# Sums of the exponentials in a local attention: from a VectorE pass to ScalarE's accumulator output

## The reference, cut to what matters

```python
def local_attention(q, k, v):            # WINDOW = 64, QK_SCALE = 8
...
    sim = jnp.einsum('bhwid,bhwjd->bhwij', bq, bk)
    mask = (i < j) | (i > j + WINDOW) | (j == -1)
    sim = jnp.where(mask, -jnp.finfo(sim.dtype).max, sim)
    attn = jax.nn.softmax(sim, axis=-1)
    out = jnp.einsum('bhwij,bhwjd->bhwid', attn, bv)
def _layer(x, ...):
    q, k, v = jnp.split(shift_token(x) @ wqkv, 3, axis=-1)   # then heads
    q, k = rotary_xpos(l2norm(q) * qs, l2norm(k) * ksc)
    x = x + local_attention(q, k, v) @ wo
    h = layernorm(shift_token(x)) * lg + lb
    a, g = jnp.split(h @ w1 + b1, 2, axis=-1)
    return x + (a * gelu(g)) @ w2 + b2
```

## Time and profile before

| | us |
|---|---|
| median of 3 runs | 4474.85 |
| lowest, highest | 4472.83, 4477.2 |
| the profiled execution's own time | 4476.7 |
| its span in the trace | 4475.0 |
| mean granted TensorE clock | 0.975 of full speed |

### The profile page before, as it was taken

One profiled execution on the slowest core, in us unless ns is written; L12 is line 12 of the kernel. 1 busy time (PEld: TensorE's weight loads), 2 busy tenths in 40 slices (PEclk: granted clock), 3 DMA queues, 4 the chain that ended last, 5 costly groups with the idle time before them and its releaser, 6 DMA issues. The chain is left out here.

```text
span 4475.0 us, 110467 instructions
## 1 busy us (share of the span) xinstructions
PE 4064.2 (91%) x35464; PEld 3177.9 (71%) x35464; DVE 2950.7 (66%) x7412; ACT 2773.7 (62%) x6382; POOL 1789.5 (40%) x1808
## 2 busy tenths in 40 slices
PE   6888799999799997879999786999999998998999
PEld 4666588888566665756666565888888886775777
DVE  5777655555399997459999554555555547775665
ACT  5666455555499997349999532555555556775333
POOL 3322122222289997028888301333333331111444
PEclk9999899999899999999999998999999999999999
DMA  0000000000000000000000000000000000000000
GB/s 15 9 8 9 19 7 6 6 6 6 17 15 16 15 16 19 27 25 17 16 16 16 23 24 17 1 0 0 0 0 0 0 2 5 3 3 18 12 12 12
DMA packets 138633, 49.26 MB, mean 11 GB/s; under 512 B 105066, under 2 KB 137644, under 8 KB 138540
## 3 DMA queue, kind: packets, MB, share of 16 engines
q1 hardware_dynamic: 138540, 48.06, 4.3%
HBM read 18.72 MB, written 4.19 MB: 5 GB/s over the span
## 5 line engine op out<-in xcount | busy, mean ns | idle before, releaser
L1155 POOL TENSOR_TENSOR l_rc<-l_rc,l_rs 128x1024 f32<-128x1024 f32 x128 | 303.4, 2371 | 118.8 <-DVE l_rs L1356 115.5
L1229 ACT ACTIVATE l_prob<-l_prob,l_mx 128x128 f32<-128x128 f32 x1024 | 311.8, 388 | 0.0
L1725 POOL TENSOR_TENSOR mb_r<-mb_r,mb_projb 128x128 f32<-128x128 f32 x64 | 84.8, 1325 | 503.0 <-DVE mb_xn L1981 503.0
L783 POOL TENSOR_TENSOR ca_prob<-ca_prob,ca_sm 128x1232 f32<-128x1232 f32 x64 | 143.9, 2249 | 299.7 <-DVE ca_sm L949 299.7
L1254 PE MATMUL l_qk_ps<-l_wqkv,l_hT 128*128 128x512 f32 x512 | 248.6, 609 | 12.9 <-DVE l_rs L1356 11.4
L1841 PE MATMUL mb_bc_ps<-mb_xT,mb_wbc 128*128 128x128 f32 x2048 | 256.6, 280 | 1.8 <-ACT mb_xT L1748 1.8
L1140 POOL TENSOR_TENSOR l_prob<-l_prob,l_sm 128x1024 f32<-128x1024 f32 x128 | 242.8, 1897 | 16.4 <-DVE l_sm L1342 15.6
L1123 POOL TENSOR_TENSOR l_rc<-l_rc,l_ss 128x1024 f32<-128x1024 f32 x128 | 243.4, 1902 | 12.6 <-POOL l_rc L1155 4.6
L1841 PEld LDWEIGHTS mb_bc_ps<-mb_xT,mb_wbc 128*128 128x128 f32 x2048 | 241.8, 194 | 2.3 <-ACT mb_xT L1748 2.3
L1868 PE MATMUL mb_x_ps<-mb_wx,mb_xT 128*128 128x256 f32 x1024 | 231.6, 379 | 0.0
L1447 ACT ACTIVATE m_gl<-m_ps,m_b 128x256 f32<-128x256 f32 (+1 forms) x192 | 76.2, 468 | 227.6 <-PE m_ps L1466 227.6
(11 more groups left out here) (367 smaller groups left out, 12055.2 us busy)
## 6 DMA issues: line engine op xcount, KB each, us to landing
l_h<-lt_y SPq DMA_DIRECT2D x256, 32.0 KB
m_hin<-lt_hn SPq DMA_DIRECT2D x64, 128.0 KB, 2.0
l_h<-lt_y SPq DMA_DIRECT2D x256, 31.8 KB
la_xin<-in_x SPq DMA_DIRECT2D x64, 64.0 KB
out_x<-k_x SPq DMA_DIRECT2D x64, 64.0 KB, 1.5
ca_ctxT<-in_ctx_T SPq DMA_DIRECT2D x128, 19.2 KB, 2.0
l_wqkv<-in_L_ffn_wqkv SPq DMA_DIRECT2D x2, 768.0 KB
ca_ctx<-in_ctx SPq DMA_DIRECT2D x64, 19.2 KB
```

The source lines that it names most:

```text
L783: gp.tensor_tensor(prob[b.slot][:], prob[b.slot][:], sm[b.lane][:, 1].unsqueeze(2).to_broadcast([T, H, S]), ALU.mult).then_inc(*pool_prob. ...
L1155: gp.tensor_tensor(wide(rc[l][:]), wide(rc[l][:]), wide(rs[l][:]), ALU.add).then_inc(*pool_sum.did("rot"))
L1229: ex = sc.activation(p[:, a, j], p[:, a, j], ACT.Exp, bias=mx[l][:, a, j:j + 1])
```

## The change

The 8 exponential activations of a batch each get an accumulator output: the sum along the 128 keys goes to one column of `sm`. VectorE's reduction over 128x1024 and its wait on itself are gone; the reciprocal now waits for the exponentials directly. ScalarE waits in addition for the reciprocal of two batches ago, since it now writes `sm` itself.

```diff
-        vec_sum = Stage(m.sem("vec_sum"), "sum rsum")
+        vec_sum = Stage(m.sem("vec_sum"), "rsum")
...
                         sc.wait_ge(*vec_max.at("max", b))
+                        sc.wait_ge(*vec_sum.at("rsum", b, ago=2))
                         for a in (0, 1):
                             for j in range(PAIRS):
-                                ex = sc.activation(p[:, a, j], p[:, a, j], ACT.Exp, bias=mx[l][:, a, j:j + 1])
+                                ex = sc.activation(p[:, a, j], p[:, a, j], ACT.Exp, bias=mx[l][:, a, j:j + 1],
+                                                   accum_out=sm[l][:, 0, PAIRS * a + j:PAIRS * a + j + 1])
                         ex.then_inc(*act_exp.did("exp"))
...
                         v.wait_ge(*act_exp.at("exp", b))
                         v.wait_ge(*pool_prob.at("norm", b, ago=2))
-                        v.tensor_reduce(sm[l][:, 0], prob[b.slot][:].rearrange("p a j t -> p (a j) t"), AX, ALU.add
-                                        ).then_inc(*vec_sum.did("sum"))
-                        v.wait_ge(*vec_sum.at("sum", b))
                         v.reciprocal(sm[l][:, 1], sm[l][:, 0]).then_inc(*vec_sum.did("rsum"))
```

## The result

The changed kernel takes 4538.67 us (median of 4 runs, 4537.58 to 4542.29) against 4475.2 us before, a ratio of 1.0143 (95% interval 1.0126 to 1.0161): 63 us slower. The forecast was 4553 us, slower. The span of the profiled execution grew from 4475.0 to 4535.9 us.

A forecast was written before the change was run, and what follows sets the result against it. A two-step loop through four engines was taken to set the step, ScalarE just behind. Removal at nothing and eight readouts per batch gave 64 x (0.69 + 0.53) = +78 us on 4474.85: 4553 us, range 4505 to 4700.

The forecast's parts named there:

- ScalarE's room, not the shares of the profile's page: Both attention stretches: four engines nearly full, ScalarE with 0.19 and 0.35 us to spare per step, despite TensorE's 91% overall.
- The removal at nothing: VectorE's sum reduction, 1209 ns per batch, some 155 us busy: only cover for a wait, so removing it gains nothing.
- e = 0.11 us from L1181's passage through the queue: Time each of eight accumulator outputs per batch adds to ScalarE's queue, taken from a 128x1 instruction: 0.11 us.
- Rivals A and B: Accumulator readout on ScalarE: A, serial, up to 0.298 us each, 4746 us, chance 0.13; B, free, 4475 us, chance 0.09.
- Two instructions: Accumulator output as main instruction plus accumulator read: documented for VectorE, unshown for ScalarE, counted as speaking against the change.
- The loop in layer 0: Loop through ScalarE, VectorE, GpSimd and TensorE, 16.84 us per two steps, sets the step; forecast 8.40 + 0.44 = 8.84.
- ScalarE's floor of 8.21 and 7.84: ScalarE's own time per step, layers 0 and 1: work plus waits for its own results; forecast to rise to 9.09 and 8.72.
- the two-step loop: Four-engine loop holding one set of exponentials per two steps; forecast in layer 1 to grow from 8.18 to 8.62 us.
- One sign of being right: In both attention stretches ScalarE is busy over 49.2 us of 50 and no longer waits at L1207.
- the 78: Forecast total growth in us: 64 batches in each layer, 0.69 us per step in layer 0 and 0.53 in layer 1.
- No loss of clock: TensorE thins to 87% busy in layer 0's longer step; the granted clock was expected to stay at 1.00.
- no cost of the new wait: ScalarE's wait for the reciprocal of two batches ago: that reciprocal comes nearly 12 us earlier, so costed at nothing.

The follow-up runs named there:

- run 2: Kernel before without VectorE's sum pass and without accumulator outputs, reciprocals taken of a constant 1: 4474.14 us, ratio 0.9997.
- run 1: Kernel before plus accumulator outputs on all eight exponentials that nobody reads; VectorE keeps its pass, no new ScalarE wait: 4538.72 us, ratio 1.015.
- Run 4: Changed kernel with ScalarE's copy of v moved behind the first small activation (Relu): 4507.28 us, ratio 1.0077 to the kernel before.
- Run 5: Kernel before with ScalarE's copy of v moved behind the first small activation (Relu), no accumulator outputs: 4458.51 us, ratio 0.9958.

## Why the prediction was right, and where not

- *ScalarE's room, not the shares of the profile's page.* Right: the two stretches decide, and there 86 us more on ScalarE weighed more than 148 us less on VectorE.
- *The removal at nothing.* Right, shown twice: run 2 (gift alone, 0.9997) and run 1 (price alone, same time as the change).
- *e = 0.11 us from L1181's passage through the queue.* Right in kind, 18% too large: 0.093. The row was the right neighbour, an unpointered 128x1 output in a pipelined sequence. By the estimate from the Trainium skill's page "Perfetto Trace Analysis", section "Optimizing Scalar/DVE Operations" (93 ns), the sum came to +61; the trace agrees, at 0.093 and 61 us. Rivals A and B fall: the reading overlaps both its neighbours, and it isn't free.
- *Two instructions.* What the page "VectorE: DVE Perf Modes" of the Trainium skill, section "Two Vector instructions with no wait between them", says of VectorE, the trace shows for ScalarE too, with 1024 rows of the reading. The Trainium skill's page "ScalarE activation tables: per-element evaluation and per-set limits", section "What a function is on this engine", says "with the same operands the instruction costs the same"; the prediction left open whether that takes in an output more. Here the ACTIVATE alone costs the same, 389 against 388 ns, and the output is an instruction of its own.
- *The loop in layer 0.* Right in kind. 8.39 + 4 x 0.093 = 8.76 and ScalarE without a gap come out nearly together, at 8.80.
- *ScalarE's floor of 8.21 and 7.84: wrong, the step of the sum that failed.* It counted busy time plus the idle time that remains. But when ScalarE waited at L1207, the copy of kT had its whole tail counted as busy. The timeline of ScalarE in layer 0, before:

```profile
1452.78 0.59 ACT L1204 ACTIVATE l_kT<-l_turn_ps 128x512 f32<-128x512 f32 x1
1453.58 0.60 ACT L1207 ACTIVATE l_val<-l_v_ps 128x512 f32<-128x512 f32 x1 [0.21 <-PE l_v_ps L1276]
```

and after (the copy of v is at 1452.48, shown under 4):

```profile
1452.00 0.61 ACT L1204 ACTIVATE l_kT<-l_turn_ps 128x512 f32<-128x512 f32 x1
```

Between the two starts lie 0.80 us with the wait and 0.48 us without. The slack there was 0.32 us, where the row shows 0.21. In layer 0 the true floor is about 8.80 - 0.74 = 8.06, so with the measured e the forecast would have been 0.15 us per step too high (+0.55 against +0.40). In layer 1 the floor was at most 8.74 - 0.32 - 0.74 = 7.68, not 7.84.
- *Layer 1: the one-step loop through TensorE was missed.* The uneven steps of the kernel before, 8.00 and about 8.33 or 8.42, were the sign: two things took turns, and the mean of 8.18 hid the one that grows twice as fast. With e measured the forecast would have been +0.40, 0.16 too low. Run 4 shows this loop: with the Relu's 0.33 us out of it layer 1 of the changed kernel falls by 0.34 us per step. Run 5 shows the two-step loop in the same way, 0.17 us per step. One sign of being right that the prediction named failed with it: in layer 1 ScalarE is busy only 48.20 of 50 and still waits at L1207.
- The two misses cancel, so with the right e the sum would have been +61, and the time looks better understood than it was; that is luck. The surplus of e makes the 78.
- *No loss of clock, no cost of the new wait.* Both right: 1.00, and run 1 has no such wait.

## What to carry to other kernels

Before moving work between two engines that both look full, find the loop that sets the step and count how often per round each engine's piece lies in it; here a pass outside all loops was worth nothing to remove (155 us), and 0.74 us per step added inside cost 0.40 and 0.555, what the slack and the rounds of the loops left of it. Steps that alternate in length can mean two loops in turn, each of which grows by its own rule, as in layer 1 here; but a loop of two steps can alternate by itself (layer 0 of run 2, 8.11 and 8.72 us towards its end, its transposes always behind GpSimd), so look in each kind of step for what the last wait is for. An accumulator output is one more instruction per output on ScalarE, so for short rows (128 elements here: 0.093 on 0.293 us, 32%) one long reduction on another engine can be the better bargain; here a reordering, which adds no work, was better than either. And a wait can hide under the tail of the instruction in front: compare the start with the end of what was waited for, not only "idle before".

## What the runs showed of the hardware

- ACTIVATION_READ_ACCUMULATOR, 128x1: 190 ns in the rows, 0.093 us of the queue behind a 128x128 ACTIVATE.
- A ScalarE instruction that waits for the one just before it costs far more than its idle time shows: 0.37 us between starts (128x16, layer 0) against 0.20 with independent work between, with 0.03 us of idle time in the profile.
- ScalarE's wait for TensorE can show as no idle time at all or nearly so: in run 4, layer 1, the copy of v starts 0.04 us behind the end of the projection and 0.12 us later than its queue would let it, and the window shows 49.51 of 50 busy.
- Moving a small activation from behind such a wait to in front of it took 0.33 us out of a loop of two steps and gained 19 us of 4478 without any change of work.
